# Linear attention in a four-layer kernel: norms moved behind the solve, keys behind the sixth column, pair-inverse products parted, masks ahead of the fourth convolution

## Reference, cut to what matters

```python
q = short_conv(x @ Wq, conv_wq)      # 4-tap convolution over time, then silu; the same for k and v
q = l2norm(q) * dk ** (-0.5)
k = l2norm(k)
# per token and head:
S = S * jnp.exp(gt)[..., None, None]
pred = jnp.einsum('bhk,bhkv->bhv', kt, S)
delta = (vt - pred) * bt[..., None]
S = S + jnp.einsum('bhk,bhv->bhkv', kt, delta)
o = jnp.einsum('bhk,bhkv->bhv', qt, S)
# then
o = o * jax.lax.rsqrt(jnp.mean(o * o, -1, keepdims=True) + EPS) * norm_weight
o = o * jax.nn.silu(gate)
return o.reshape(b, t, VALUE_DIM) @ Wo
```

## Time and profile before

| | us |
|---|---|
| median of 3 runs | 1369.48 |
| lowest, highest | 1358.34, 1372.09 |
| profiled execution | 1379.87 |
| its span | 1378.3 |
| rest of it, outside the span | 1.57 |
| the seven steady intervals from one `seeds` to the next | 308.3 |

### The profile page before, as it was taken

One profiled execution on the slowest core, in us unless ns is written; L12 is line 12 of the kernel. 1 busy time (PEld: TensorE's weight loads), 2 busy tenths in 40 slices (PEclk: granted clock), 3 DMA queues, 4 the chain that ended last, 5 costly groups with the idle time before them and its releaser, 6 DMA issues. The chain is left out here.

```text
span 1378.3 us, 26691 instructions
## 1 busy us (share of the span) xinstructions
PE 1182.4 (86%) x10170; PEld 994.0 (72%) x10170; DVE 871.2 (63%) x2570; ACT 622.7 (45%) x1591; POOL 81.4 (6%) x90
## 2 busy tenths in 40 slices
PE   4999999899999974999899998358888898868478
PEld 3888789788878863888789887246766677657255
DVE  3767375375737657666656665698787887673423
ACT  4635454353445433434243432447575765534111
POOL 1000000000000001000000001200122111200000
PEclk9999999999999986999999996679798997777689
DMA  8010000000000020000000001100000000000322
GB/s 278 1 62 1 1 1 1 0 0 0 0 1 1 1 85 1 1 1 1 3 1 0 1 1 48 53 26 4 28 28 27 2 29 28 2 1 2 104 69 95
DMA packets 25730, 34.12 MB, mean 25 GB/s; under 512 B 4780, under 2 KB 21004, under 8 KB 25612
## 3 DMA queue, kind: packets, MB, share of 16 engines
q1 hardware_dynamic: 25612, 32.52, 7.3%
HBM read 30.34 MB, written 2.17 MB: 24 GB/s over the span
## 5 line engine op out<-in xcount | busy, mean ns | idle before, releaser
L986 PE MATMUL b_ps<-ln_high,b_high 128*128 128x512 f32 x256 | 101.9, 398 | 26.3 <-PEq L61 20.9
L333 DVE TENSOR_REDUCE a_negmax<-a_ps 128x1 f32<-128x128 f32 x128 | 37.3, 291 | 115.3 <-PE a_ps L514 106.7
L986 PE MATMUL b_ps<-ln_low,b_high 128*128 128x512 f32 x256 | 101.6, 397 | 0.0
L986 PE MATMUL b_ps<-ln_high,b_low 128*128 128x512 f32 x256 | 101.5, 396 | 0.0
L889 DVE TENSOR_TENSOR gate_up_raw<-gate_up_raw,b_ps 128x512 f32<-128x512 f32 x64 | 43.2, 686 | 91.4 <-PE b_ps L986 59.3
L553 PE MATMUL a_ps<-a_wo_high,a_oT 128*128 128x256 f32 x512 | 94.8, 283 | 1.9 <-DVE a_oT L359 1.9
L1013 PE MATMUL b_ps<-b_wd_high,b_mid 128*128 128x256 f32 x512 | 96.4, 283 | 0.0
L945 ACT ACTIVATE gate_up_raw<-b_ps 128x512 f32<-128x512 f32 x64 | 37.5, 599 | 120.6 <-PE b_ps L986 120.5
L477 PE MATMUL a_ps<-ln_high,a_w_high 128*128 128x512 f32 x160 | 69.1, 432 | 14.9 <-PEq L61 14.9
L553 PEld LDWEIGHTS a_ps<-a_wo_high,a_oT 128*128 128x128 f32 x512 | 79.7, 189 | 2.8 <-DVE a_oT L359 2.8
L1013 PEld LDWEIGHTS b_ps<-b_wd_high,b_mid 128*128 128x128 f32 x512 | 80.6, 188 | 0.6
(11 more groups left out here) (376 smaller groups left out, 3061.8 us busy)
## 6 DMA issues: line engine op xcount, KB each, us to landing
d_slots<-in_D_packed SPq DMA_DIRECT2D x16, 433.0 KB, 4.4
c_a_all<-a_scratch SPq DMA_DIRECT2D x8, 768.0 KB, 3.8
x<-in_hidden SPq DMA_DIRECT2D x4, 512.0 KB, 10.1
a_raw<-in_A_q SPq DMA_DIRECT2D x4, 512.0 KB, 7.9
gate_up_raw<-in_A_o SPq DMA_DIRECT2D x1, 2048.0 KB, 13.9
gate_up_raw<-in_B_g SPq DMA_DIRECT2D x1, 2048.0 KB, 12.1
gate_up_raw<-in_B_u SPq DMA_DIRECT2D x1, 2048.0 KB, 8.2
b_wd<-in_B_d SPq DMA_DIRECT2D x1, 2048.0 KB, 10.0
```

The lines of the kernel that those rows point to most:

```text
L986: mm = nc.tensor.matmul(ps[:, bank, :], wpart, xpart, start=(j == 0), stop=(j == len(passes) - 1))
```

## The change

Only the order of steps changes, and one helper is parted in two; no arithmetic is added or removed. On PE `all_norms(c)` goes from behind `known` to right behind the solve, ahead of `new_state`; `turn_keys` goes ahead of `pair_part`, and `pair_inverses` is emitted before `turn_values`, its second group (`pair_inverses_turned`) after them. On ACT `silu(c, 2)` and `all_squares(c)` go ahead of `place_corner` and the copies of y, and the table load with `norm_roots(c)` goes ahead of the taps 4 and 5. On DVE the masks `off_diagonal` go ahead of `keep_state` (two of them ahead of the fourth group of convolution steps), columns 2, 3 and 4, 5 go ahead of `keep_state` and `second_values`, `keys(c)` goes from behind column 13 to behind column 6, and convolution step 14 to ahead of column 10.

```diff
                     for h in range(3, DH):
                         run(c, scan, h)
+                    run(m, off_diagonal, 0)
+                    run(m, off_diagonal, 1)
                     run(c, convolve, 9, 12)
+                    run(m, off_diagonal, 2)
+                    run(m, columns, 2, 4)
                     run(s, keep_state)
-                    run(m, off_diagonal, 0)
-                    run(m, columns, 2, 3)
-                    run(m, off_diagonal, 1)
-                    run(m, columns, 3, 4)
-                    run(m, off_diagonal, 2)
-                    run(m, columns, 4, 5)
+                    run(m, columns, 4, 6)
                     run(s, second_values)
-                    run(m, columns, 5, 9)
+                    run(m, columns, 6, 7)
+                    run(c, keys)
+                    run(m, columns, 7, 8)
                     run(c, convolve, 12, 13)
-                    run(m, columns, 9, 10)
+                    run(m, columns, 8, 9)
                     run(c, convolve, 13, 14)
                     run(s, mean_square, 0)
+                    run(m, columns, 9, 10)
+                    run(c, convolve, 14, 15)
                     run(m, columns, 10, 11)
-                    run(c, convolve, 14, 15)
...
-                    run(m, columns, 13, 14)
-                    run(c, keys)
-                    run(m, columns, 14, 16)
+                    run(m, columns, 13, 16)
                     run(m, seeds)
...
+                    if inside(c):
+                        channels.silu(act, c, 2)
+                    run(c, all_squares)
                     run(s, place_corner)
                     run(s, copy_y, 0)
                     run(s, copy_y, 1)
-                    if inside(c):
-                        channels.silu(act, c, 2)
                     run(s, solved_keys)
-                    run(c, all_squares)
                     run(s, copy_wkT)
+                    if inside(m):
+                        nc.scalar.preload_act_table_set("natural_log_exp_and_others")
+                    run(c, norm_roots)
                     if inside(c):
                         channels.tap(act, c, 4)
                         channels.tap(act, c, 5)
                     run(s, squares, 0)
                     run(s, save_output, 0)
-                    if inside(m):
-                        nc.scalar.preload_act_table_set("natural_log_exp_and_others")
-                    run(c, norm_roots)
...
                     mm.then_inc(S["a_done"], 1)
+
+                def pair_inverses_turned(b):
+
                     for u in range(UNITS):
                         for rows in QUARTERS[0:3]:
...
+                    run(m, turn_keys)
                     run(s, pair_part)
-                    run(m, turn_keys)
                     run(m, scores, 2)
+                    run(s, pair_inverses)
                     run(m, turn_values, 0)
                     run(m, turn_values, 1)
-                    run(s, pair_inverses)
+                    run(s, pair_inverses_turned)
...
                     run(s, solve, 0)
                     run(s, solve, 1)
+                    run(c, all_norms)
                     run(s, new_state)
                     run(s, turn_solved_keys)
                     run(s, outputs, 0)
                     run(c, job, 4)
                     run(c, job, 5)
                     run(s, known)
-                    run(c, all_norms)
                     run(s, outputs, 1)
```

## The result

| | before | changed |
|---|---|---|
| median, us | 1366.63 (4 runs) | 1404.62 (4 runs) |
| lowest, highest | 1358.34, 1372.09 | 1398.97, 1411.61 |
| profiled execution | 1379.87 | 1398.97 |
| its span | 1378.3 | 1397.4 |
| ratio | | 1.0286, interval 1.0203 to 1.0369 |

The change makes the kernel 2.9% slower: 38 us by the medians, 19 by the two profiled executions. The changed kernel's four runs lie near 1399 and near 1410, so that a difference of under some 10 us from its median of 1404.62 is not told from none. The forecast was 1374.0 with a range of 1355 to 1390: the measured time lies outside, on the slow side.

A forecast was written before the change was run, and what follows sets the result against it. Bound: a chain changing engines, DVE from `second_values` to `seeds`, then PE and ACT through joins, `place_corner` and solve. Terms -3.6 + 2.4 + 2.0 + 0.7 = +1.5 us per iteration, +4.5 together; forecast 1374.0 us, range 1355 to 1390.

The forecast's parts named there:

- Front: From first instruction of `seeds` to second join: 6.8 us instead of 10.4, a gain of 3.6, or 2.1 at low clock.
- the clock term: PE's low clock at the front, costing 1.5 us where it comes; half taken, 0.7 us lost per iteration.
- My own second rival: Clearly slower: PE waits 3.6 us for `seeds`, low clock every iteration costs 1.5, collisions more; +3.5 each, 1388 us; chance 0.21.
- The corner: `place_corner` on ACT waits behind `silu(c, 2)` and the squares: 2.3 us later, and the solve with it.
- the term I had put at nothing: Low clock from PE's new gap before the solve: no charge, since the solve already had it at times.
- POOL: POOL's multiplies beside DVE's column products: 1.7 us, plus 0.3 for `decayed_keys` and `queries`; 2.0 us lost per iteration.
- Norm roots and `keys`: Roots done near 1048, DVE at `keys` near 1049.5: no wait, by a margin of 1 us.
- Masks and columns ahead: DVE steps moved into earlier waits: masks buy nothing, column 5 gains 0.6 us; DVE waits about 2.5 at `second_values`.
- My own sign of being wrong: Wrong if column products stay under 0.6 us, the corner isn't late, or the period moves by more than 3 us.
- The first rival: POOL's multiplies miss the column products and the clock stays up at the front: -0.7 us per iteration, 1357 us; chance 0.24.

The follow-up runs named there:

- the fifth experiment: Changed kernel plus four spare matmuls on PE between `turn_keys` and `pair_part`; 1386.63 us, 1.0160 times the kernel before.
- the ninth experiment: The kernel before, unchanged, run again for a second trace; 1369.09 us.
- the second experiment: Changed kernel with POOL's `gated_outputs` held until `seeds` of the next batch are done; 1385.99 us, 1.0118 times the kernel before.
- the twelfth experiment: Changed kernel plus four spare matmuls on PE between `turn_low(m, 2)` and the solve; 1397.64 us, 1.0230 times the kernel before.
- The fourth: Kernel before with pair-inverse products parted, `turn_keys` ahead of `pair_part` and `keys(c)` behind column 8; 1383.99 us, 1.0111 times the kernel before.
- The seventh experiment: Changed kernel with `all_norms(c)` back behind `known`, nothing else; 1410.59 us, 1.0329 times the kernel before.
- eight: Kernel before with pair-inverse products parted, `turn_keys` ahead, `keys(c)` behind column 10 and POOL's `gated_outputs` held for next `seeds`; 1358.64 us, 0.9942 times.

## Why the prediction was wrong

**Front: the mechanism held, its size and its clock did not.** The new leg at full clock was right: the fifth experiment's best legs, 6.22 and 6.35 us, are even under my 6.8. But the 3.6 us were the distance from it to an old leg of 10.4 at the low clock, so most of them were clock and not order. At the full clock the old leg takes 6.96 us (the ninth experiment) and the gain is 0.6; at the low clock on both sides I had 2.1 and 1.97 was measured. So the step that failed first is the clock term: I priced the low clock at half its cost, as if it would come in every second iteration. It came in every one (8.2 to 8.9 us in all), and PE idled for 2.4 to 3.2 us before `pair_part` in the six. I had worked out 3.6 for that gap. That this gap brings the low clock is shown only in part, by the fifth experiment, while the second has it with gaps of 0.5 to 1.4. My own second rival named this mechanism and its price, 1.5 us per iteration, and the rows for it were there: a gap of 2.58 us had been followed by the low clock. Half was a compromise, not a reading. The gap of 1.61 us in front of the jobs, which wait for `add_out`, I did not see at all.

**The corner: right, 2.3 us forecast, 2.20 measured.** What I left out was what the gap of 2.3 us that it opens in front of the solve does to what runs next. I wrote that the solve had had the low clock at times already and charged nothing. But the norms now stand right behind the solve, inside the low stretch: 2.63 us instead of the 1.4 I used. The leg grew by 1.66 us where I had 0.7, and the twelfth experiment gives 2.6 back in the four iterations where filling that gap keeps the clock. That is the term I had put at nothing.

**POOL: right in sum.** Forecast 2.0, measured 2.2 against a leg of 12.64 (13.22 less the moved column, 0.58), of which the second experiment gives back 1.65. Both multiplies fell on column products, each for 0.8 us, not one for 1.6 as in the earlier trace rows. `decayed_keys`, for which with `queries` I had 0.3, cost a third product 0.54 us, in the second experiment too. As the Trainium skill, GPSIMD Engine Reference, section Key points, has it, POOL and VectorE contend over VectorE's instructions with two SBUF inputs. The trace agrees, with 1.24 us for 0.40. The fourth and seventh experiments show a case within the same 0.3, `keys` against `queries`: 0.75 us when both are released by the same step of ACT.

**Norm roots and `keys`: right.** `keys` followed column 6 without a wait, at 1105.80, 1.25 us after ACT's last root. The seventh experiment, with later norms, shows the wait of 1.60 us that this margin kept away.

**Masks and columns ahead: right.** They only moved DVE's waiting: it stands for 2.36 us before `second_values`, where I had about 2.5, and for 3.29 before `keep_state`.

**The sum: two errors.** Per iteration I had +1.5 and the earlier trace rows's 44.2 us became 47.7: +3.5. My own sign of being wrong, a period that moves by more than 3 us, came. Of the missing 2.0, 0.9 are the clock at the front, 0.9 the clock at solve and norms, and 0.2 POOL. Over six iterations that is 12 us and would have given 1386. In the two traces iterations 1 to 6 together took 20.7 us more (I had 7), iteration 7 took 3.8 less (2.5), and the first `seeds` came 2.3 later (nothing). The second error is larger, the other 19 of the 38 us: the traced execution of the kernel before lay 13.2 us above its median of four runs, that of the changed kernel 5.7 below its own. The second of these stays open. As to the first, I took the profiled execution's periods as the kernel's and moved the difference to the median. In its second trace, of 1369.09 us, the kernel before takes 39 to 42 us in four of six iterations, since the low clock comes and goes in it; the changed kernel, in both of its traces, takes over 46 us in every one of the six. A change that fixes the clock at its lower level must be priced against the better executions of before, not against the one that was traced.

**The rivals.** The second, clearly slower, is nearest to what happened: the low clock at the front in every iteration. I gave it 0.21. That its price per iteration, +3.5, is the measured one to the tenth is luck. Its gap of 3.6 us was 2.4 in most iterations, under the 2.6 from which it was to decide, and its collisions were 2.2 and not 3.2 in all; the low clock at solve and norms filled the place. Its time, 1388, is 17 us short. The first rival's parts, held clock and missed collisions, are what eight shows in part when they are arranged.

## What to carry to other kernels

When a step moves ahead on one engine, list what every other engine does in the moment it is released: an in-order queue turns a wait that was harmless at its end (a silu) into a late solve when it moves to the front, and a POOL multiply that ran beside PSUM work into a stall of DVE when it runs beside products of two SBUF tensors. A shorter path that leaves PE idle for 2 us in front of its work may give the gain back through the clock, as here at the solve, so price the PE work behind each new gap at both clocks. Compare a leg before and after at the same clock, or the clock is counted as a gain of the order. And take the terms from more than one trace where the clock moves an iteration by 4 us.

## What the runs showed of the hardware

A DVE product of two SBUF tensors that met a running POOL multiply ended behind it in every row here: 0.40 us became 1.24, 1.65 and 2.01, and the end fell within 0.3 us behind POOL's in each. Sums, which read one tensor, kept their length beside the same multiply (0.29 and 0.54 us).

Work that computes nothing can pay: four spare matmuls, 1.99 us of PE's time, in a gap of 2.4 us made the changed kernel 18 us faster. Eight of them, which don't fit (9 us), and four before the solve (7) are not told from none. In the changed kernel's first trace PE idled for 2.18 or 2.19 us in front of the solve in five iterations, and in each the granted clock fell to 0.50 within that gap. Before, it fell behind a gap of 2.57 to 2.59 us in front of scores in eight of ten (both traces). The Trainium skill, TensorE: Matmul & The Clock Gate, section "HAM oscillation — how this bites in real kernels", says that PE falls back to the half clock over idle gaps and pays for each anew. The traces agree for most of these gaps and not for all: two of the ten in front of scores were not followed by it.
